# Preparing output tiles 0 to 2 inside the last attention group, with projection 0 right behind the last score

## The reference

```python
def layernorm(x): return (x - mean(x)) / sqrt(var(x) + 1e-5)
h = layernorm(x)
q, k, v = split(clip(h @ Wqkv.T, -8, 8))
q, k = layernorm(q) * q_w + q_b, layernorm(k) * k_w + k_b     # over all 512
scores = q @ k.T / 4 + slope[head] * (pos_k - pos_q)           # causal
att = softmax(scores) @ v                                      # 32 heads
x = x + att @ Wout.T
x = x + layernorm(x) @ sum(alphas * bases, axis=0).T           # 4 matrices of +-1
```

## Time and profile before

| what | us |
|---|---|
| median of three runs | 710.57 |
| the profiled execution, its own time | 710.61 |
| its span in the trace | 708.9 |
| around the span | 1.7 |
| PE busy | 674.5 (95%) |
| DVE busy | 575.5 (81%) |
| ACT busy | 410.3 (58%) |
| POOL busy | 313.2 (44%) |

### The profile page before, as it was taken

The page is one execution under the profiler, slowest core; times in us unless marked ns, Lnnn a source line. Parts: engine busy times, 40 slices in busy tenths (PEclk is TensorE's granted clock), DMA queues, the critical chain, the costliest instruction groups (busy, mean ns, idle before and its releaser), DMA issues.

```text
span 708.9 us, 16007 instructions
## 1 busy us (share of the span) xinstructions
PE 674.5 (95%) x6096; PEld 413.3 (58%) x6096; DVE 575.5 (81%) x990; ACT 410.3 (58%) x855; POOL 313.2 (44%) x403
## 2 busy tenths in 40 slices
PE   3999999997999999999999999999999995799998
PEld 2888888884344554555455445545544431588886
DVE  6899999997999999999999999999999700367664
ACT  5132332333069887788788778878878894222221
POOL 1367766777132634626427422322232234544440
PEclk9999999997579999999999999999999999799999
DMA  8225666767945443333334334433433211544541
GB/s 303 76 61 175 179 179 187 201 192 224 289 113 134 123 128 101 115 115 106 118 108 120 108 112 123 105 108 109 130 107 105 77 26 41 154 133 131 159 146 62
DMA packets 102060, 93.64 MB, mean 132 GB/s; under 512 B 11640, under 2 KB 81912, under 8 KB 101984
## 3 DMA queue, kind: packets, MB, share of 16 engines
q1 hardware_dynamic: 97856, 86.84, 41.9%
q10 hardware_dynamic: 2016, 3.67, 1.9%
q0 software_dynamic: 2112, 2.10, 1.3%
HBM read 57.44 MB, written 33.82 MB: 129 GB/s over the span
## 4 chain that ended last, share of the span: by engine, by line
PE 73%; DVE 15%; issue 7%; POOL 2%; DMA 2%; ACT 1%; SPq 0%; DVEq 0%; POOLq 0%; ACTq 0%
PE ps L1104 23%; PE ps L1139 20%; PE ps L1084 9%; PE ps L1018 6%; PE ps L1020 5%; PE ps L1019 5%; DVE stats L957 4%; PE ps L1026 2%; DVE qk_stat L902 2%; DVE qk L898 2%; PE ps L1080 2%; DVE x_stat L868 1%; DVE xt_lo L861 1%; DVE rest L877 1%; DVE v_ext L911 1%
## 5 line engine op out<-in xcount | busy, mean ns | idle before, releaser
L957 DVE TENSOR_REDUCE stats<-ps 128x1 f32<-128x512 f32 (+3 forms) x608 | 358.3, 656 | 31.6 <-PE ps L1084 29.3
L787 ACT ACTIVATE probs<-ps 128x512 f32<-128x512 f32 (+2 forms) x640 | 309.0, 559 | 71.2 <-PE ps L1104 71.0
L1084 PE MATMUL ps<-first_k,first_q 54*128 54x128 bf16 (+3 forms) x1152 | 217.3, 282 | 5.1 <-DVE stats L957 4.5
L1104 PE MATMUL ps<-second_q,second_k 64*128 64x128 bf16 (+4 forms) x1152 | 204.6, 273 | 0.0
L1104 PE MATMUL ps<-first_q,first_k 54*128 54x512 bf16 (+3 forms) x768 | 193.8, 328 | 0.1
L679 POOL TENSOR_SCALAR_AFFINE_SELECT probs<-probs 128x256 f32<-128x256 f32 x256 | 103.0, 408 | 130.5 <-ACT probs L787 123.4
L1139 PE MATMUL ps<-probs,v_sb 128*32 128x512 f32 (+3 forms) x1536 | 157.0, 496 | 1.6 <-issue 0.8
L1104 PEld LDWEIGHTS ps<-first_q,first_k 54*128 54x128 bf16 x768 | 57.6, 94 | 110.5 <-ACT probs L787 107.6
L1084 PEld LDWEIGHTS ps<-first_k,first_q 54*128 54x128 bf16 x1152 | 92.3, 96 | 51.0 <-DVE stats L957 36.0
L1104 PEld LDWEIGHTS ps<-second_q,second_k 50*128 50x128 bf16 (+1 forms) x1152 | 91.7, 95 | 21.0 <-issue 0.6
L1018 PE MATMUL ps<-wqkv_hi,xt_hi 128*128 128x512 f32 x192 | 76.9, 401 | 0.0
(11 more groups left out here) (79 smaller groups left out, 824.4 us busy)
## 6 DMA issues: line engine op xcount, KB each, us to landing
parts_dram<-parts SPq DMA_DIRECT2D x48, 256.0 KB, 4.2
v_dram<-v_ext SPq DMA_DIRECT2D x16, 512.0 KB, 4.0
v_sb<-v_dram SPq DMA_DIRECT2D x16, 512.0 KB, 4.4
o_dram<-o_sb SPq DMA_DIRECT2D x32, 256.0 KB
first_q<-parts_dram SPq DMA_DIRECT2D x96, 64.0 KB
first_k<-parts_dram SPq DMA_DIRECT2D x96, 64.0 KB
second_q<-parts_dram SPq DMA_DIRECT2D x96, 64.0 KB
second_k<-parts_dram SPq DMA_DIRECT2D x96, 64.0 KB
```

Of the source, the lines that this page charges most:

```text
L787: act.activation(weights, scores, ACT.Exp, scale=SCALE).then_inc(exp_done, 1)
L957: dve.tensor_reduce(to, scores, AX.X, ALU.max).then_inc(max_taken, 1)
L1084: last = pe.matmul(ps[:, bank, r * cols:(r + 1) * cols], first_q[n % STACKS][rows, hp, i * P:(i + 1) * P], first_k[n % STACKS][rows, hp, k ...
L1104: return pe.matmul(ps[:, bank, r * cols + first:r * cols + last], stack_k[n % STACKS][rows, heads[r] // PAIR, kb * P:(kb + 1) * P], stack_ ...
```

## The change

Six things are moved; no arithmetic is added or taken away.

1. PE runs projection 0 at step 640 (`PROJ_AT`), behind the last score and ahead of the weighing of the last three units; projections 1 and 2 follow that weighing, and turn 0, turn 1 and product 0 come behind projection 2. The wait for `o_ready` 32 goes.
2. ACT makes `att_hi` of tiles 0 and 1 at steps 617 and 619 and of tile 2 at step 641.
3. POOL makes `att` of tiles 0, 1 and 2 at steps 613, 615 and 622 and `att_lo` of tiles 0 and 1 at 618 and 620.
4. POOL makes the four low chunks of the feed-forward weight in group 14 (`LOW_AT`, steps 573 to 582).
5. SP loads the sums of batch 0, the residual rows of tiles 0 to 2, and the tiles themselves ahead of the last three stores to `o_dram`, and waits for fewer of those stores.
6. DVE's `invert(0)` keeps its place in DVE's order.

```diff
+LOW_AT = [(GROUPS - 2) * NE + 13 + 3 * c for c in range(DC)]
+LAST_GROUP = (GROUPS - 1) * NE
+AHEAD = 2
+ATT_AT = [LAST_GROUP + 13, LAST_GROUP + 15, LAST_GROUP + 22]
+ATT_HIGH_AT = [LAST_GROUP + 17, LAST_GROUP + 19, GROUPS * NE + 1]
+ATT_LOW_AT = [LAST_GROUP + 18, LAST_GROUP + 20]
+PROJ_AT = GROUPS * NE
...
 # sync, group_step
                 if s == GROUPS - 2:
-                    load_sums(0)
-                if s == GROUPS - 1:
-                    store_inverses(0)
-
-                    sp.wait_ge(inv_stored, 16)
+
                     sp.wait_ge(wout_ready, DC)
                     sp.wait_ge(wffn_ready, DC)
+                    load_sums(0)
                     for t in range(3):
-                        if t == 2:
-                            sp.wait_ge(att_ready, 1)
+                        load_residual(t)
+                    store_inverses(0)
+                    sp.wait_ge(inv_stored, 16)
+                    for t in range(AHEAD):
                         load_sums_of_tile(t)
-                        load_residual(t)
+                    sp.wait_ge(att_ready, 1)
+                    load_sums_of_tile(AHEAD)
...
-                    sp.wait_ge(o_stored[half], 16 * (GROUPS if b else GROUPS - 1 - half))
+                    sp.wait_ge(o_stored[half], 16 * GPB * (b + 1))
...
 # gpsimd, exp_step and output_step
+                    if s == LOW_AT[c]:
+                        low_chunk(wffn_lo, wffn_sum, wffn_hi, wffn_hi_ready, wffn_ready, c)
+                if s in ATT_AT:
+                    attend(ATT_AT.index(s))
+                if s in ATT_LOW_AT:
+                    low_attention(ATT_LOW_AT.index(s))
...
             run_steps(pool, exp_step)
-            for c in range(DC):
-                low_chunk(wffn_lo, wffn_sum, wffn_hi, wffn_hi_ready, wffn_ready, c)
...
+                if AHEAD < t < TILES:
+                    attend(t)
+                if AHEAD <= t < TILES:
+                    low_attention(t)
...
 # scalar, exp_step and output_step
-                if s == GROUPS * NE:
-                    high_attention(0)
...
+                if s in ATT_HIGH_AT:
+                    high_attention(ATT_HIGH_AT.index(s))
...
-                if 1 <= t < TILES:
+                if AHEAD < t < TILES:
                     high_attention(t)
...
 # tensor, exp_step and output_step
+                if s == PROJ_AT:
+                    pe.wait_ge(max_taken, NTAKE * GROUPS)
+                    project(0)
...
-            pe.wait_ge(o_ready, 2 * GROUPS)
...
+                if s == -2:
+                    project(1)
+                    project(2)
+                elif AHEAD < t < TILES:
+                    project(t)
```

More of the change, by code:

```diff
@@ L519, in group_step @@
                 if s == GROUPS - 2:
+                    sp.wait_ge(wout_ready, DC)
+                    sp.wait_ge(wffn_ready, DC)
                     load_sums(0)
-                if s == GROUPS - 1:
+                    for t in range(3):
+                        load_residual(t)
                     store_inverses(0)
                     sp.wait_ge(inv_stored, 16)
-                    sp.wait_ge(wout_ready, DC)
-                    sp.wait_ge(wffn_ready, DC)
-                    for t in range(3):
-                        if t == 2:
-                            sp.wait_ge(att_ready, 1)
+                    for t in range(AHEAD):
                         load_sums_of_tile(t)
-                        load_residual(t)
+                    sp.wait_ge(att_ready, 1)
+                    load_sums_of_tile(AHEAD)
             def load_sums_of_tile(t):
@@ L680, in exp_step, with attend, low_attention @@
                                            pattern=[[0, 2], [1, P]], channel_multiplier=-1).then_inc(masked, 1)
+            def attend(t):
+                pool.wait_ge(o_loaded[t % 2], 2 * 16 * (t // 2 + 1))
+                if t >= 2:
+                    pool.wait_ge(att_lo_ready, t - 1)
+                pool.tensor_tensor(att[t % 2][:], o_in[t % 2][:],
+                                   inv_in[t % 2][:].rearrange("p (a t) -> p a t", a=1).broadcast_to([P, DC, P]),
+                                   ALU.mult).then_inc(att_ready, 1)
+            def low_attention(t):
+                pool.wait_ge(att_hi_ready, t + 1)
+                pool.tensor_tensor(att_lo[t % 2][:], att[t % 2][:], att_hi[t % 2][:].bitcast(F32),
+                                   ALU.subtract).then_inc(att_lo_ready, 1)
             run_steps(pool, exp_step)
-            for c in range(DC):
-                low_chunk(wffn_lo, wffn_sum, wffn_hi, wffn_hi_ready, wffn_ready, c)
             def output_step(s):
                 t = s + 3
[L689 to L698, removed]
+                if AHEAD < t < TILES:
+                    attend(t)
+                if AHEAD <= t < TILES:
+                    low_attention(t)
             run_outputs(pool, output_step)
@@ L928, in exp_step @@
                                       ALU.max).then_inc(max_joined, 1)
-                if s == (GROUPS - 1) * NE:
+                if s == LAST_GROUP - EARLY + 1:
                     invert(0)
@@ L1173, in exp_step, with project @@
                         weigh(e // NE * NU + u)
+            def project(t):
+                if t == 0:
+                    pe.wait_ge(wout_ready, DC)
+                pe.wait_ge(att_lo_ready, t + 1)
+                if t >= 2:
+                    pe.wait_ge(x2_ready, t - 1)
+                product(ps[:, O_BANK[t % 2], :], att_hi[t % 2], att_lo[t % 2], wout_hi, wout_lo).then_inc(proj_done, 1)
             run_tiles(pe, tile_step, -1, TILES - 1)
```

## The result

| | before | after |
|---|---|---|
| median of runs on one chip | 711.45 us (4 runs, 710.38 to 713.24) | 701.68 us (4 runs, 701.3 to 701.7) |
| profiled execution, its span | 710.61, 708.9 us | 701.69, 700.0 us |
| mean granted TensorE clock, share of full | 0.966 | 0.973 |

The ratio of the times is 0.9866, with a 95% interval of 0.9852 to 0.988. The change saves 9.8 us by the medians and 8.9 us in the profiled executions, where 12.1 were forecast. The time is at the upper edge of the range, and outside the likeliest case's own range.

What follows compares the result with a forecast made beforehand. PE bounds the output stage, after an 11.7 us hole. Hole 11.7, half clock 2.85, waits 0.5: 15.0, less 0.6 (ACT), 1.1 (feed-forward 0), 1.3 (turn 2): 12.0; by leads, 12.4 less 0.3: 12.1 off 710.61, 698.5 us; range 696.7 to 701.8.

Steps and rivals of the forecast that it cites:

- likeliest case: The forecast itself: 698.5 us, its own range 697.3 to 699.7 us, chance 0.57.
- Tiles 0 and 1: POOL, group 15: inverses stored at 573.4 land by 576.4; `att` 0 starts 580.3, done 581.6; `att` 1 done 582.9.
- Rival (b): Inverses land late (5.6 us or behind the residual loads), ACT waits in front of exp: 2.3 us more, 700.8; chance 0.14.
- ACT: Group 15: rounding of tile 0 at about 581.8 without a wait, 0.6 us ahead of the copy, making PE 0.6 late.
- PE behind the last score: Last score ends 593.9, projection 0 at once at full clock; feed-forward 0 at 606.0, lead 13.6; PE idles 1.1 us.
- The last store: Last store to `o_dram`, issued 599.3, takes 5.3 to 7.5 us; DVE's wait puts feed-forward 1 at 612.1 to 614.3.
- up to 1.0, but it falls into the same time as the DVE wait, so I add nothing: PE's wait for `att_lo` 3 (607.5 to 609.8) at projection 3, due 608.8; priced at nothing.
- Rival (c): The clock falls in the chopped start, PE idling 0.6, 1.1 and 1.3 us: 2.85 us more, 701.4; chance 0.09.
- Tile 5: Its load follows the first output store and hangs on a `y_out` 1.9 us later against PE's stream: 0.3 us lost.
- Rival (a): Last store to `o_dram` lands in 4 us or less: feed-forward 1 at 611.95, lead 13.6, 697.0 us; chance 0.15.
- (d): Slower than before: ACT's wait for `att` at step 617 stops exps, scores and weighings; 713.4 at 12 us late; chance 0.03.
- (e): The change does nothing: projections wait as before, or another wait takes the hole's place: 710.6 us; chance 0.02.

## Why the prediction was wrong, step by step

**Tiles 0 and 1: right, and earlier than said.** The store of the inverses landed 1.7 us after its issue where I had 3.0; `att` 0 started at 579.29, not 580.3. Nothing waited for it. The cost of the low chunks is nowhere to be seen: no engine's wait names them. Rival (b), late inverses, is out.

**ACT: right in kind, short in size.** The rounding met no wait (581.88 against 581.8). But the copy came 0.57 us later, PE's wait for it grew from 0.37 to 0.88, and a wait of 0.25 for an exp came at 588.36; the last score ended near 594.35 instead of 593.9. With this feed-forward 0 started at 606.46 and not at 606.0: 0.46 us. Late roundings gave 0.47 back.

**PE behind the last score: right.** Projection 0 ran at once at full clock, PE idled 1.05 us ahead of feed-forward 0 (forecast 1.1).

**The last store: right in time, wrong in who pays.** I had 5.3 to 7.5 us for it; it took 7.3 from issue to the sums' issue. DVE idled 2.60 us for the sums, in the band named (0.5 to 3). But it isn't what PE waits for.

**The step that failed: "up to 1.0, but it falls into the same time as the DVE wait, so I add nothing".** I had the load of tile 3 behind the store, `att_lo` 3 at 607.5 to 609.8 and a need at 608.8. It was ready at 611.77, and PE's wait of 2.37 us for it is the last of the signs that the prediction named for being wrong (over 1 us). The reasoning held only for its size: a delay of up to 1.25 us, the price of the DVE wait, does fall into the same time, since DVE's wait delays what PE wants behind projection 3 (turn 2 and the low part of tile 1) and POOL's delays projection 3 itself. But the 609.8 took the load as prompt once the store was through, which it was by 606.87. Yet the load's last 256 packets had begun only beside the store's last ones and were through at 608.39, 1.5 us later: `att` started 8.4 us after the load's issue, and `att_lo` 3 was ready 2 us past my bound. At that size POOL's wait covers DVE's, not the other way round. Against the forecast, from feed-forward 0 to 1:

| | us |
|---|---|
| forecast, 606.0 to 613.2: PE's own 5.95, wait 1.25 | 7.2 |
| measured, 606.46 to 616.62 | 10.16 |
| PE's own work, as before | 5.93 |
| half clock in projection 3 (4.81 less 3.21) | 1.60 |
| the wait, what is left (2.37 of it between the modelled ends) | 2.63 |

So 1.38 us by a longer wait, 1.60 by the clock, 0.46 from ACT, less 0.02 in PE's own work: 3.42, which is the difference of 613.2 and 616.62. That the clock fell is in part luck, as it did so in three of four executions. Both removals show the rest. With tile 3's load moved ahead the wait and the fall went together, and 3.7 us came back; with the wait filled only the clock's share came back, 1.65.

**Rival (c) came in part, as a consequence of that wait.** I gave the clock's fall 0.09 as an alternative to the forecast, at 2.85 us, and argued against it that the clock had fallen after 4.3 us without a matmul (the 0.55 granted in the us from 599 puts it nearer 3.9). It fell after idle times of 1.05 and 2.37 us with 3 us of full work between them, and cost 1.60; with the second one filled it did not fall. It was no alternative to the waits but their follow-on cost. The Trainium skill, "TensorE: Matmul & The Clock Gate", section "HAM oscillation", tells of a kernel whose pieces of work are shorter than the waits between them, and whose clock falls again at each of them. This trace agrees in that the clock fell behind a wait (0.50 granted from 613 on), but here the work of 3 us was longer than the wait of 2.37. So with waits of 0.6 to 1.3 us the prediction's "by that rule it would be this rival" took more from the page than it states.

**Tile 5: 0.3 priced, none seen in after** (83.38 against 83.34 us from feed-forward 1 on); with tile 3's load first it was 0.24.

**The gain itself was priced well:** the hole of 11.7 went, and half clock in it was worth 2.46 in one execution and 1.98 in another, not 2.85. Rival (a) could not decide alone, as the store did not land early. Made to, by the cut, it gave 697.4 where rival (a) said 697.0. Rivals (d) and (e) are out.

Why the load behind the store needed 7.2 us: three quarters of `o_in` passed beside the store, and 256 packets waited until the store's began to run out, while 12 of 16 engines stood idle (share 0.25). That they waited in line on the store's four engines is the reading that fits this count, the share and the cure by the cut; the trace names no engine for a packet. The kernel with tile 3's load ahead of the last store shows the same split behind the store of the first half (issued by 585.3): 384 packets by 589, none until 591, then 256. There nobody waits for them.

## What to carry to other kernels

When work is pulled ahead of a wait, look in every queue for what stands just behind the last transfer of the stage before: it now has a deadline that the old hole had hidden (here it took back 3 of the 12 us forecast). A wait priced at nothing because a longer one covers it is free only up to the length of that cover: bound its own size from both sides, and let the clock's fall follow from it as a further cost. For a transfer, look at its outermost dimension, at the DMA share beside it and at what stands right behind it in the queue, and don't price it by its bytes alone.

## What the runs showed of the hardware

- A store of 256 KB whose slowest dimension is 4 kept the DMA share at 0.26 and took 5.9 us alone (tile 3's load ahead of it) and 7.3 with a load behind it; cut in four along that dimension it landed in 3.1 us from its first issue, at a share of 0.54. The stores of the output tiles in after, also of 256 KB but with a slowest dimension of 128, land in 2.1 us (median of 16). The Trainium skill, "DMA: Bandwidth & Descriptors", section "Why a DMA increments its semaphore by 16 and not by 1", says that a transfer is spread over the largest number of engines up to 16 that divides the slowest dimension of both sides. That is 4 here; by that rule the share would be 0.25, and the trace agrees with 0.26.
- A load of 640 packets issued right behind that store moved 384 of them within 2 us and began the other 256 only beside the store's last packets; it was through 7.2 us after its issue. So what stood behind the store was held up in part, while the DMA share was 0.25.
- The granted clock fell at 613 with no idle time longer than 2.37 us shortly before it, in three executions of four, and nine matmuls in that idle time, which nobody needed, kept it whole in four of four and took 1.65 us off the tail.
